# Cross attention in a two-layer decoder: a second pass of context scores with the keys on partitions, in place of transposed probabilities

## The reference

```python
# per sequence b, heads h = 0..31 of width 16; q, k, v from Wq, Wk, Wv; rotary q, k for the tokens
own = masked_softmax(q_h @ k_h.T) @ v_h                # 112 x 112 scores
ctx = softmax(q_h @ ck_h.T) @ cv_h                     # 112 x 375 scores
o_h = own + tanh(gate_h) * ctx
x   = x + concat(o_h) @ Wo
```

## Time and profile before

| | |
|---|---|
| median of 3 runs | 1815.8 us (1813.87 to 1819.28) |
| the profiled execution | 1809.46 us, its span 1807.7 us, clock 0.991 |
| PE busy | 1743.7 us, 96% of the span |
| DVE, ACT, POOL busy | 979.6, 609.9, 406.5 us |
| HBM traffic | 172.36 MB, mean 95 GB/s |

### The profile page before, as it was taken

The page is one execution under the profiler, slowest core; times in us unless marked ns, Lnnn a source line. Parts: engine busy times, 40 slices in busy tenths (PEclk is TensorE's granted clock), DMA queues, the critical chain, the costliest instruction groups (busy, mean ns, idle before and its releaser), DMA issues.

```text
span 1807.7 us, 31468 instructions
## 1 busy us (share of the span) xinstructions
PE 1743.7 (96%) x12998; PEld 1155.4 (64%) x12998; DVE 979.6 (54%) x1865; ACT 609.9 (34%) x1934; POOL 406.5 (22%) x485
## 2 busy tenths in 40 slices
PE   7999999999999999999999999998999999999998
PEld 6776666646566665665665888886587765444444
DVE  3775656427656566666744111116555555665887
ACT  1242222316655555555740111110422223332411
POOL 2532222512020120120003000005142220002576
PEclk9999999999999999999999999999999999999999
DMA  9100002000000000000215988877000031762001
GB/s 397 37 1 1 1 1 111 1 10 18 18 18 18 2 18 18 2 18 2 117 48 206 390 331 327 332 266 258 1 1 1 2 120 68 276 197 96 17 24 41
DMA packets 31838, 172.36 MB, mean 95 GB/s; under 512 B 4008, under 2 KB 4008, under 8 KB 17904
## 3 DMA queue, kind: packets, MB, share of 16 engines
q1 hardware_dynamic: 29456, 163.01, 24.0%
q0 software_dynamic: 2240, 7.34, 1.2%
HBM read 155.66 MB, written 16.52 MB: 95 GB/s over the span
## 4 chain that ended last, share of the span: by engine, by line
PE 86%; DVE 9%; POOL 3%; ACT 2%; issue 1%; DMA 0%; POOLq 0%; DVEq 0%; SPq 0%; ACTq 0%
PE PS L1209 8%; PE PS L1001 6%; PE PS L1356 6%; PE PS L1052 5%; PE PS L1278 5%; PE PS L1086 5%; PE PS L1125 4%; PE PS L1077 4%; PE PS L1387 4%; PE PS L1218 4%; PE PS L1323 3%; PE PS L1109 3%; PE PS L1374 3%; PE PS L1145 2%; PE PS L1060 2%; PE PS L1040 2%
## 5 line engine op out<-in xcount | busy, mean ns | idle before, releaser
L2159 POOL TENSOR_TENSOR rstd<-veps,mhalf 128x1 f32<-128x1 f32 (+1 forms) x71 | 53.7, 757 | 498.2 <-DVE veps L1417 475.0
L1209 PEld LDWEIGHTS PS<-R,W 128*128 128x128 f32 x1344 | 153.2, 192 | 11.7 <-issue 11.7
L1541 DVE TENSOR_REDUCE nmx<-PS 112x2 f32<-112x750 f32 x128 | 114.3, 933 | 77.9 <-PE PS L1109 77.5
L1209 PE MATMUL PS<-R,W 128*128 128x128 f32 x1344 | 153.6, 275 | 2.2 <-DVE R L1713 2.2
L2012 ACT ACTIVATE R<-PS,nmx 112x375 f32<-112x375 f32 x256 | 142.9, 575 | 4.1 <-DVE nmx L1541 4.1
L1001 PE MATMUL PS<-xT,W 128*128 128x224 f32 x640 | 127.6, 360 | 0.9 <-ACT xT L1943 0.7
L1001 PEld LDWEIGHTS PS<-xT,W 128*128 128x128 f32 x640 | 122.4, 194 | 9.1 <-issue 6.9
L1720 DVE TENSOR_TENSOR R<-R,PS 128x512 f32<-128x512 f32 x21 | 14.4, 687 | 199.1 <-PE PS L1209 199.1
L1356 PE MATMUL PS<-W 128*128 128x512 f32 x256 | 117.5, 602 | 0.0
L1125 PEld LDWEIGHTS PS<-cst,R 112*125 112x125 f32 x768 | 90.1, 191 | 22.0 <-issue 17.5
L1387 PE MATMUL PS<-W,xT 128*128 128x512 f32 x224 | 100.7, 593 | 1.9 <-ACT xT L1953 1.9
(11 more groups left out here) (301 smaller groups left out, 3230.1 us busy)
## 6 DMA issues: line engine op xcount, KB each, us to landing
W<-in_we SPq DMA_DIRECT2D x63, 1024.0 KB, 7.8
W<-in_entwT SPq DMA_DIRECT2D x8, 1024.0 KB, 7.3
W<-in_entpw SPq DMA_DIRECT2D x8, 1024.0 KB, 8.9
W<-in_ctxT SPq DMA_DIRECT2D x8, 750.0 KB, 4.2
R<-in_ctxT SPq DMA_DIRECT2D x8, 750.0 KB, 9.9
R<-in_ctx SPq DMA_DIRECT2D x8, 750.0 KB
xs_rows<-in_x SPq DMA_DIRECT2D x3, 1792.0 KB, 36.4
R<-xs_rows SPq DMA_DIRECT2D x21, 256.0 KB, 8.3
```

What stands on the lines that cost most here:

```text
L1209: o = e.matmul(PS[:, m, c * 128:(c + 1) * 128], gate_up(j % 3, k, off + c * 128), BT[:, j % 2, k, :], start=k == 0, stop=k == 3)
L1541: e.tensor_reduce(nmx[0:S, par, r:r + 2], PS[0:S, r:r + 2, 0:SC], AX.X, ALU.max, negate=True).then_inc(*up("cmax", (b, c, par, r)))
```

## The change

The 12 transposes of a context task and their three copies go. In their place the scores are computed a second time with the roles of the operands exchanged: `xk` multiplies 125 keys (as weights) with the 112 queries, for 3 blocks of keys and 4 blocks r, so the result already lies with keys on the partitions. The maximum must then be part of the product: `cm` writes the negated maxima into a small tile `nmw`, `mt` turns that on TensorE, VectorE adds it to a row of `QM` that is zero for this head, and the keys carry a 1 in that row (`KcT` is stored twice, once per par, by two ScalarE activations). `ce` is now two exponentials without bias and without sums, straight to the operand of `xcv`. The sums come from the value matmuls: the padding of `VX` and `Vc` is 1 in place of 0, so the unused 16 of each 32 output rows hold the sum. `xd` (VectorE and GpSimd) and `xn` (VectorE) then normalize each (b, c) on their own; `xr` and `xb` go. `ck` and `cv` are cut into two halves (`ck1`, `cv1` first), which can lie in two gaps.

```diff
-        "pj": 1.55, "vx": 1.75, "ck": 2.55, "cv": 3.5, "xs": 0.45, "xc": 0.65, "xt": 0.42, "xct": 0.45,
+        "pj": 1.55, "vx": 1.75, "ck": 1.28, "ck1": 1.28, "cv": 1.75, "cv1": 1.75, "xs": 0.6, "xc": 0.85, "xk": 0.8, "mt": 0.12, "xt": 0.45,
...
 def context(b):
-    return [("ck", b, c) for c in range(4)] + [("cv", b, t) for t in range(3)]
+    return [(k + z, b, c) for k, n in (("ck", 4), ("cv", 3)) for c in range(n) for z in ("1", "")]
...
+SHARE = (1.5, 1.2, 1.0, 1.5)
...
+    for n in range(4 * NBATCH + 2):
+        here, last, past = (pieces_of(m) for m in (n, n - 1, n - 2))
+        a, b_, c_, d = [], [], [], []
+        if here:
+            a += [("xs", *here)] + [("xm", *here, k) for k in range(2)]
+        if last:
+            a += [("xk", *last, 1)] + [("ce", *last, 1, r) for r in (0, 2)] + [("xv", *last, par) for par in range(2)] + [("xcv", *last, 0)]
+        if here:
+            a += [("xm", *here, 2), ("xe", *here)]
+            b_ += [("xc", *here, 0)] + [("cm", *here, 0, r) for r in (0, 2)]
+        if past:
+            b_.append(("xn", *past))
+        if last:
+            c_ += [("xcv", *last, 1), ("xu", *last)]
+        if here:
+            c_ += [("xc", *here, 1), ("mt", *here, 0)] + [("cm", *here, 1, r) for r in (0, 2)]
+            d += [("xt", *here, par) for par in range(2)] + [("xk", *here, 0)] + [("ce", *here, 0, r) for r in (0, 2)]
+        if last:
+            d.append(("xd", *last))
+        out += [a, b_, c_, d]
...
+            if n % 4 == 3:
+                some.insert(1, ("mt", *pieces_of(n // 4), 1))
+            k = 3 if n % 4 == 0 else len(runs[n])
+            out += runs[n][:k] + some[:k < len(runs[n])] + runs[n][k:] + some[k < len(runs[n]):]
...
     if k == "xs":
         return (0, 1, 2, 3), 4, [("masked", a)] * 4
     if k == "xc":
-        return (0, 1, 2, 3), 4, [("cexp", (*a, r)) for r in range(4)]
+        return (0, 1, 2, 3), 4, [("cmax", (*a, r)) for r in (0, 0, 2, 2)]
+    if k == "mt":
+        return LOW, 1, [("shifted_q", a)]
+    if k == "xk":
+        return (0, 1, 2, 3), 4, [("cexp", (*a, r)) for r in (0, 0, 2, 2)]
...
+            def mt(b, c, par):
+                m = bank(("mt", b, c, par))
+                w.wait_ge(*at("cmax", (b, c, par, 2)))
+                e.transpose(PS[:, m, 0:S], nmw[0:S, par, :], ident[0:S, 0:S]).then_inc(*up("max_turned", (b, c, par)))
+
+            def xk(b, c, par):
+                z, i = (b // UB) % 2, b % UB
+                w.wait_ge(*at("shifted_q", (b, c, par)))
+                for t in range(3):
+                    for r in range(4):
+                        if t == 0:
+                            free(("xk", b, c, par), r)
+                        ro = slice(32 * r, 32 * r + 32)
+                        o = e.matmul(PS[0:KC, r, bcol(t)], KcT[b % 2][par][ro, c, t * KC:(t + 1) * KC], QM[z][ro, c, par, bcol(i)],
+                                     start=True, stop=True)
...
-            def xct(b, c, par, t_):
-                m = bank(("xct", b, c, par, t_))
-                for r in range(4):
-                    w.wait_ge(*at("cexp", (b, c, par, r)))
-                    t = e.transpose(PS[0:KC, m, bcol(r)], p_of(b, c, par)[0:S, r, t_ * KC:(t_ + 1) * KC], ident[0:S, 0:S])
-                t.then_inc(*up("p_turned", ("xct", b, c, par, t_)))
...
+            def mt(b, c, par):
+
+                q = QM[(b // UB) % 2][:, c, par, bcol(b % UB)]
+                w.wait_ge(*at("max_turned", (b, c, par)))
+                e.tensor_tensor(q, q, PS[:, bank_of["mt", b, c, par][0], 0:S], ALU.add).then_inc(*up("shifted_q", (b, c, par)))
+
+            def xd(b, c):
+
+                low, high_ = C("parity")[:, 0:1], C("parity")[:, 1:2]
+                w.wait_ge(*at("ou", (b, c)))
...
+                e.tensor_scalar(ND[:, 1, :], OU[:, c % 2, 0, :], high_, None, ALU.mult).then_inc(*own())
+                settled()
+                e.scalar_tensor_tensor(ND[:, 1, :], OU[:, c % 2, 1, :], low, ND[:, 1, :], ALU.mult, ALU.add).then_inc(
+                    *up("denom", (b, c)))
+                w.wait_ge(*at("denom", (b, c)))
+                e.stream_shuffle(ND[:, 2, :], ND[:, 1, :], PAIRS).then_inc(*own())
+                settled()
+                e.reciprocal(ND[:, 2, :], ND[:, 2, :]).then_inc(*own())
...
+            def ck(b, c):
+                w.wait_ge(*at("context", ("ck", b, c)))
...
+                for par in range(2):
+                    e.activation(KcT[b % 2][par][:, c, :], PS[:, bank_of["ck", b, c][0], 0:SC], ACT.Identity,
+                                 bias=C("unit")[:, par:par + 1], scale=C("keep")[:, par:par + 1]).then_inc(
...
+            def ce(b, c, par, r):
+                w.wait_ge(*at("scores", ("xk", b, c, par, 3)))
+                e.activation(p_of(b, c, par)[0:KC, r:r + 2, :], PS[0:KC, r:r + 2, 0:3 * S], ACT.Exp).then_inc(
+                    *up("cexp", (b, c, par, r)))
```

More of the change, by code:

```diff
@@ L1 @@
+import itertools
 from contextlib import ExitStack
@@ L146, in constants @@
     add("halfpi", np.full((128, 1), np.pi / 2))
+    unit = p[:, None] % 32 == 16 - 16 * np.arange(2)[None, :]
+    add("keep", ~unit)
+    add("unit", unit)
     return np.ascontiguousarray(np.concatenate(parts, 1))
 HALVES = [j + 8 if j % 16 < 8 else j - 8 for j in range(32)]
+PAIRS = [(j + 16) % 32 for j in range(32)]
 CONSTS = constants()
@@ new lines, with pieces_of @@
+SHARE = (1.5, 1.2, 1.0, 1.5)
+def pieces_of(n):
+    if not 0 <= n < 4 * NBATCH:
+        return None
+    return n // 4, n % 4
+def attendx():
+    out = []
+    for n in range(4 * NBATCH + 2):
[18 more added lines that the diff above has]
+        out += [a, b_, c_, d]
+    for b in range(1, NBATCH):
+        out[min(16 * (b + 1) + 6, len(out) - 1)] += [("xw", b - 1), ("stats", 2, b - 1)]
+    return out
@@ L307, in cross @@
 def cross():
-    out, gaps = [], attendx()
+    out, runs = [], attendx()
     for b in range(NBATCH):
@@ L321, in cross @@
         late = expert_rows(range(5)) if b == NBATCH - 1 else []
-        mine = range(12 * b, 12 * b + 12)
-        whole = sum(cost(s) for s in fill + late) + sum(cost(s) for n in mine for part in gaps[n] for s in part)
-        unit = whole / sum(GAP[TASKS[n][2]] for n in mine)
+        mine = range(16 * b, 16 * b + 16)
+        unit = sum(cost(s) for s in fill + late) / (4 * sum(SHARE))
         due = 0.0
         for n in mine:
-            if n == mine[2]:
+            if n == mine[3]:
                 fill += late
-            out.append(("xs" if TASKS[n][2] == "own" else "xc", *TASKS[n][:2], *TASKS[n][2:][:TASKS[n][2] != "own"]))
-            due += unit * GAP[TASKS[n][2]]
-            head, tail = gaps[n]
-            due -= sum(cost(s) for s in head + tail)
+            due += unit * SHARE[n % 4]
             some = []
@@ L336, in cross @@
                 some.append(fill.pop(0))
-            out += head + some + tail
+            if n % 4 == 3:
+                some.insert(1, ("mt", *pieces_of(n // 4), 1))
+            k = 3 if n % 4 == 0 else len(runs[n])
+            out += runs[n][:k] + some[:k < len(runs[n])] + runs[n][k:] + some[k < len(runs[n]):]
     h = part(range(5))
-    at_end = {("xcv", 7, 3, 1, 2): h[:1], ("xr", 7): h[1:2], ("xb", 7): h[2:4], ("xw", 6): h[4:6]}
-    for head, tail in gaps[len(TASKS):]:
-        for s in head + tail:
-            out += [s] + at_end.get(s, [])
+    at_end = {("xk", 7, 3, 1): h[:1], ("xcv", 7, 3, 1): h[1:4], ("xw", 6): h[4:6]}
+    for s in itertools.chain(*runs[16 * NBATCH:]):
+        out += [s] + at_end.get(s, [])
     return out
@@ L641, in place @@
     taken, frees = [-1] * 8, [None] * 8
-    late = False
+    late, held = False, None
     for n, step in enumerate(order):
@@ L646, in place @@
         may, count, events = psum_use(step, late)
+        if step[0] in ("ck", "cv"):
+            taken[bank[step][0]], held = n, None
         if not count:
             continue
-        got = list(may) if len(may) == count else sorted(may, key=lambda m: (taken[m], m))[:count]
-        bank[step] = got
+        got = list(may) if len(may) == count else sorted(may, key=lambda m: (m == held, taken[m], m))[:count]
+        if step[0] in ("ck1", "cv1"):
+            held = got[0]
+        bank[step] = bank[{"ck1": "ck", "cv1": "cv"}.get(step[0], step[0]), *step[1:]] = got
         past[step] = [] if group else [frees[m] for m in got if frees[m]]
@@ L945, in program @@
         lp_slot = {s: n % 4 for n, s in enumerate(lps)}
[L946 to L947 removed]
+        pxs = [s for s in order if s[0] == "xt"]
+        px_of = {s: PX[n % 4] for n, s in enumerate(pxs)}
         rts = [s[1:] for s in order if s[0] == "pj"]
@@ L1137, in xv @@
                 o.then_inc(*up("values", ("xv", b, c, par)))
-            def xcv(b, c, par, t_):
-                s = ("xct", b, c, par, t_)
-                w.wait_ge(*out_of(s, turned_by(s)))
-                w.wait_ge(*out_of(("cv", b, t_), t_))
-                for r in range(4):
-                    h = (8 * c + 2 * r + par) * 32
```

(3 more changed lines are left out.)

300 lines of the change are left out of this document (109 added, 191 removed), and 1 row of the table COST.

## The result

| | before | after |
|---|---|---|
| median of 9 runs | 1815.8 us (1812.29 to 1820.85) | 1806.65 us (1801.98 to 1810.58) |
| ratio, 95% interval | 1 | 0.9947 (0.9930 to 0.9964) |
| span of the profiled execution | 1807.7 us | 1803.3 us |
| first own scores to last `xw` | 533.2 us | 525.2 us |

The change makes the kernel 9.2 us faster, where 24.7 were forecast. The direction was right, the size was not.

What follows compares the result with a forecast made beforehand. TensorE was taken to bound cross attention: -42.2 us of its own work and +17.5 of waits and half clock give -24.7, from 1815.8 to 1791 us (chance 0.56). Its own range was 1777 to 1805, the stated range 1768 to 1818.

Steps and rivals of the forecast that it cites:

- `xk` at 0.82 us: Second scores on TensorE: 64 bursts of 24 records add 52.5 us; bounds 0.59 and 0.89 us a burst.
- `mt` at 0.10 us, 49 cuts at 0.07: TensorE additions: 64 single transposes cost 6.5 us, and 49 projections cut in two cost at most 3.4 us.
- Waits of 42 us: TensorE waits and half clock in the stage: 18 us in 28 rounds, 24 in the last four, in place of 25.
- The long wait in front of `xk` behind the second maxima: Hand-over `xc` to `xk`: 1.6 to 2.35 us of fill wanted, nearly two thirds of 18 us of waits.
- nothing to speak of: Hand-over `xk` to `xc`: banks free after 2.57 us, TensorE has 2.5 us of work, so practically no wait.
- The last sequence: Last four rounds, with almost no fill: 20 us of waits, plus 4 us for a falling clock.
- VectorE is late: Rival, chance 0.12: VectorE's queue delays the second maxima and next mask by over 0.8 us a round; up to 1829 us.
- the 3 us that were named as a sign of being wrong: Sign against the forecast: any stage other than cross attention changing by more than 3 us.
- GpSimd beside VectorE: Both engines on the same tiles: contention could slow `xd`'s second pass, `xm` and `xn`, adding some us.
- the rival in which every round falls to 1.2 GHz: Rival, chance 0.04: TensorE's clock falls for 3 us every round, 48 us on top, 1839 us.
- One sign of being wrong: Sign against the forecast: half clock in the first seven sequences.
- The waits take it all: Rival, chance 0.12: each of five hand-overs is 0.15 to 0.2 us longer, 25 us return; 1816 us, no change.

Runs made afterwards that it cites:

- m1_seams: Changed kernel plus test bursts of each form on TensorE behind its last step, alone and alternating; a full-array and 32-row pair took 2.04 us, the parts alone 1.68.
- e2_norms: Changed kernel with the next pair's row statistics and scaling moved behind the fourth query and key projections of the fill; 1801.77 us, 0.9920 of the kernel before.
- e3_norecip: Changed kernel without the reciprocal of the sums, so its output is not normalized; 1800.74 us, 0.9920 of the kernel before.
- e6_idle: Changed kernel with 15 more matmuls in the last sequence whose result nobody reads; 1809.58 us, 0.9973 of the kernel before.
- g1_before_cut: Kernel before, with only its context projections cut into halves as in the change and dealt out by its own costs; 1842.65 us, 1.0146 of the kernel before.
- e7_shares_off: Kernel of e2_norms with the fill dealt to a round's four gaps by shares 0.8, 1.8, 1.8, 0.8; 1824.11 us, 1.0051 of the kernel before.
- e1_whole: Changed kernel with the two halves of each context projection always side by side; 1846.55 us, 1.0173 of the kernel before.

## Why the prediction was wrong in size

Forecast: -42.2 us of TensorE's own work, +17.5 of waits and half clock, -24.7 (its 42 us of waits less 25 are 17, and its own range, 18 down from 1791, would begin at 1773 and not 1777; neither matters here). Shown by the profile after: -32.9 and +24.9, so -8.0 in the stage.

- *What bounds the kernel, what goes*: right. TensorE is at 96% after as before, `xct`, `xr` and `xb` gave what was counted for them (98.3 and 13.5 us with their waits, for 95.4 and 9.2).
- *`xk` at 0.82 us*: nearly. 0.85 is the usual burst, 54.4 us for 64; 0.67 of it is work and 0.18 seams. The lower bound of 0.59 in the forecast left the seams out, and with them gone even the form itself takes 0.67.
- *`mt` at 0.10 us, 49 cuts at 0.07*: the step of the sum that failed. "At most the 0.07 us by which a burst's tail overlaps the next" reads a seam (what a burst costs more for standing beside another kind) off the overlap of two records. The price is the change between full-array and 32-row or 32-column matmuls, 0.18 us (m1_seams), in a row of bursts that changes form at nearly every step. The stage has 353 changes of form now and 296 before; 267 and 211 of them are between full-array and 32-row or 32-column matmuls, the rest between rows and columns. 56 more by 0.18 are 10 us, about what the sum was off by (9.3). By term, with waits taken out: the cut projections take 7.5 us more than whole ones, for 3.4 forecast; `mt` 9.3 us, for 6.5 (0.10 in 8 of 64 between full-array neighbours, 0.15 with a change of form on one side, 0.19 or more elsewhere); `xk` 54.4, for 52.5; `pj` and `xt`, put at no change, 1.8 and 1.4 more, and `xv` 3.3 less. A whole `ck` took 2.6 us, two halves take 2.56 to 2.92.
- *Waits of 42 us*: too few, by 9, and in other places. This is the second step that failed, and the first round's 8 us are nearly all of it; in the next 27 rounds the total was right (18) by luck. What each hand-over wants, read from the traces of both kernels, against the forecast: `xs` to `xk` 1.27 us (1.3), `xk` to `xc` 0.45 (nothing), `xc` to `xc` 0.91 (0.9), `xc` to `xk` 1.2 (1.6 to 2.35), `xk` to `xs` 1.3 (1.5). The long wait in front of `xk` behind the second maxima, two thirds of my 18 us, is 3.3 us of idle time. What I called "nothing to speak of", `xk` to `xc`, is the commonest: 0.45 us in 12 rounds, since `xv` is shorter (0.41, not 0.5) and the second exponential ends later than my 2.5. The first round's 8 us weren't in the list: I walked the hand-overs of the five users of banks 0 to 3, and not VectorE's queue, in which norms of another sequence stand (e2_norms: 4.9 us back).
- *The last sequence*: 20 us of waits and 4 of half clock forecast, some 25 found. The place and size were right, the mechanism only in part: VectorE's queue, its reciprocal above all, is on the path there (e3_norecip, 5.9 us), and it is the rival "VectorE is late", confined to one sequence of eight (and, by the norms, to the first round). A higher clock, bought with added matmuls, won nothing there (e6_idle).
- *The other engines, the transfers*: right; DVE 376.1 us against "at most 437", and GpSimd 56 us more where 44 were counted.
- *The stage ahead*: it ends 2.8 us later than in the profile before, close to the 3 us that were named as a sign of being wrong. In all eleven other profiles the first own scores start at 407.0 to 409.5 us (405.8 before), also in g1_before_cut, whose only difference up to there is the cut of the context projections that stand in that stage's fill. Either the cut costs something there too, or the profiled execution before is the exception (1809.46 us, and the nine timed ones began at 1812.29); no run tells the two apart.
- *GpSimd beside VectorE*: the shuffle and the reciprocal that run beside GpSimd's two passes took 0.40 us, as the shuffle alone before, and 1.553 where 1.51 was extrapolated. But the contention that the Trainium skill (GPSIMD Engine Reference, 1. Specifications) names for VectorE instructions with two SBUF inputs is seen in this trace, beside other GpSimd passes (L2159 and L2162 are those of the rotary embedding):

```profile
529.92 1.70 POOL L2159 TENSOR_TENSOR R<-R,cst 128x224 f32<-128x224 f32 x1
...
531.13 0.62 DVE L1552 SCALAR_TENSOR_TENSOR R<-R,tg 128x112 f32<-128x112 f32 x1
...
542.14 0.68 POOL L2162 TENSOR_TENSOR R<-R,cst 128x224 f32<-128x224 f32 x1
542.25 1.51 DVE L1515 SCALAR_TENSOR_TENSOR R<-R,sx 112x896 f32<-112x896 f32 x1
```

  Without a GpSimd pass beside them L1552 takes 0.335 us and L1515 1.09. Eighteen instructions of `xm`, `xd` and `xn` in the stage are longer so, by 5.7 us together; not all fit the rule, since the `TENSOR_TENSOR` of `xn` with two SBUF inputs keeps its 0.38 us beside GpSimd, and the small `TENSOR_SCALAR` of `xm` with one goes from 0.17 to some 0.5. VectorE has room for it in most rounds; what it costs the kernel no run isolates.
- *The clock*: in 405 to 870 us it is 0.99 in the change and in e7_shares_off too, with over 40 us of waits spread over 28 rounds. So the rival in which every round falls to 1.2 GHz is out. One sign of being wrong did come: half clock in the first sequence, behind the 3.94 us of the first round.
- *The rivals*: none is what happened. "The waits take it all" comes nearest by its number (1816), but its mechanism, every signal 0.15 to 0.2 us longer, isn't seen.

What I had in hand and did not use: the list of needs by gap. Put on e1_whole's list of steps afterwards it gives 31 to 36 us of waits more than on the change's, by the lengths taken for the fill, where 41 came; it would have told that the cut and its placement carry the gain, and that the margin of each gap, not the total of the fill, is what decides.

Open: how much of g1_before_cut's loss is the held bank; why the last sequence took 9.6 us of idle matmuls for 2.0 us and 5.1 us of projections for 4.4.
